# A four-layer graph network on one core: the first pass reordered, and the first norm's squares moved to ScalarE

## The reference

```python
# layer 0: relation weights, every row divided by its norm
rel = adj.T * (q @ k.T);  rel = rel / norm(rel, axis=2);  y = rel @ v
# layer 1: degree-normalised graph convolution
dis = where(deg > 0, rsqrt(deg), 0);  y = (adj * dis[:, None] * dis[None, :]) @ (x @ weight) + bias
# layer 2: gated recurrent update, 3 steps (in_mat = out_mat = adj)
z = sigmoid(w3(av) + u3(h));  r = sigmoid(w4(av) + u3(h))
hv = tanh(w5(av) + u5(r * h));  h = (1 - z) * h + z * hv
# layer 3: attention with 8 heads, masked by adj, output projection
x = layernorm(x + layer(x))          # after each of the four
```

## Time and profile before

| | |
|---|---|
| median of 3 timed executions | 2054.93 us (2052.94 to 2056.11) |
| the profiled execution | 2056.67 us |
| its span, first to last instruction | 2054.8 us |
| mean granted TensorE clock | 0.991 of full speed |
| busy: TensorE, VectorE, ScalarE, GpSimd | 97%, 75%, 62%, 50% |

### The profile page before, as it was taken

The page is one execution under the profiler, slowest core; times in us unless marked ns, Lnnn a source line. Parts: engine busy times, 40 slices in busy tenths (PEclk is TensorE's granted clock), DMA queues, the critical chain, the costliest instruction groups (busy, mean ns, idle before and its releaser), DMA issues.

```text
span 2054.8 us, 34581 instructions
## 1 busy us (share of the span) xinstructions
PE 1998.2 (97%) x12222; PEld 1634.8 (80%) x12222; DVE 1541.4 (75%) x3442; ACT 1277.9 (62%) x2629; POOL 1034.4 (50%) x1153
## 2 busy tenths in 40 slices
PE   6889999999999999999999999999999999999997
PEld 5767888887888878888887888888888887888775
DVE  5557777777777878777777777878777777777867
ACT  3336657576575766657576575766657576575766
POOL 3123645546365554645446365554645446364546
PEclk8999999999999999999999999999999999999999
DMA  4003022130211303122130211303122130211212
GB/s 138 1 21 73 14 60 52 42 73 22 52 42 42 73 21 72 28 56 52 42 73 22 54 40 42 73 22 72 34 50 52 42 73 21 57 37 44 71 41 73
DMA packets 65631, 101.14 MB, mean 49 GB/s; under 512 B 11440, under 2 KB 31152, under 8 KB 65456
## 3 DMA queue, kind: packets, MB, share of 16 engines
q1 hardware_dynamic: 65456, 98.87, 19.0%
HBM read 23.34 MB, written 8.39 MB: 15 GB/s over the span
## 4 chain that ended last, share of the span: by engine, by line
PE 91%; DVE 4%; ACT 3%; issue 1%; DMA 0%; POOL 0%; DVEq 0%; SPq 0%; POOLq 0%; ACTq 0%
PE ps L1066 18%; PE ps L1068 18%; PE ps L1067 17%; PE ps L1088 12%; PE ps L1185 11%; PE ps L1205 6%; PE ps L1169 5%; PE ps L1511 2%; ACT fa L570 1%; PE ps L1267 1%; DVE xn L791 1%; PE ps L1418 1%; PE ps L1359 1%; PE ps L1305 1%; ACT ra L481 0%
## 5 line engine op out<-in xcount | busy, mean ns | idle before, releaser
L341 POOL TENSOR_SCALAR fa<-fa,rsum 128x512 f32<-128x512 f32 x512 | 454.9, 900 | 54.5 <-POOL rsum L335 54.5
L335 POOL TENSOR_TENSOR rsum<-esum,mhalf 128x2 f32<-128x2 f32 x256 | 199.0, 777 | 528.5 <-ACT fa L457 526.8
L817 DVE CUSTOM_DVE_ANT_0 fa<-ps,mask 128x512 f32<-128x512 f32 x512 | 332.1, 686 | 132.4 <-PE ps L1169 130.0
L457 ACT ACTIVATE fa<-fa,nmax 128x512 f32<-128x512 f32 x512 | 367.6, 728 | 27.0 <-DVE nmax L817 27.0
L452 ACT COPY pT<-ps 128x512 f32<-128x512 f32 x480 | 277.0, 584 | 130.6 <-PE ps L1185 130.1
L1185 PE MATMUL ps<-ident,fa 128*128 128x128 f32 x1920 | 287.4, 275 | 7.9 <-ACT pT L452 5.7
L1185 PEld LDWEIGHTS ps<-ident,fa 128*128 128x128 f32 x1920 | 228.8, 140 | 80.6 <-issue 23.8
L804 DVE TENSOR_TENSOR ra<-ps,ra 128x512 fp32r<-128x512 f32 x224 | 151.2, 687 | 161.9 <-ACT ra L608 90.0
L1088 PE MATMUL ps<-adjT,ra 128*128 128x512 f32 x1024 | 253.6, 399 | 3.2 <-DVE ra L959 3.2
L1088 PEld LDWEIGHTS ps<-adjT,ra 128*128 128x128 f32 x1024 | 193.1, 191 | 46.5 <-issue 3.8
L330 POOL TENSOR_TENSOR rstd<-veps,mhalf 128x2 f32<-128x2 f32 x128 | 98.0, 772 | 166.6 <-DVE veps L767 141.5
(11 more groups left out here) (209 smaller groups left out, 4709.6 us busy)
## 6 DMA issues: line engine op xcount, KB each, us to landing
ra<-ra SPq DMA_DIRECT2D x512, 128.0 KB, 2.3
fa<-in_x_T SPq DMA_DIRECT2D x17, 512.0 KB, 4.7
fa<-in_x SPq DMA_DIRECT2D x17, 512.0 KB, 3.9
out<-fa SPq DMA_DIRECT2D x15, 512.0 KB, 3.0
fa<-in_L_gnn_w_w SPq DMA_DIRECT2D x3, 512.0 KB, 9.6
adj_n<-in_adj SPq DMA_DIRECT2D x1, 1024.0 KB, 8.9
fa<-in_L_gnn_u_w SPq DMA_DIRECT2D x2, 256.0 KB, 9.6
out<-xn SPq DMA_DIRECT2D x2, 256.0 KB, 2.1
```

The lines of the kernel that those rows point to most:

```text
L335: nc.gpsimd.tensor_tensor(rsum[:, 2 * k:2 * k + 2], esum[:, 2 * k:2 * k + 2], mhalf[:, 4:6], ALU.pow).then_inc(rs_r, 1)
L341: nc.gpsimd.tensor_scalar(SC[:, g], SC[:, g], rsum[:, 2 * k + u:2 * k + u + 1], 1.0, ALU.mult, ALU.mult).then_inc(nrm, 1)
L457: nc.scalar.activation(SC[:, s % RING], SC[:, s % RING], ACT.Exp, bias=nmax[:, s:s + 1], scale=-1.0, accum_out=esum[:, s:s + 1]).then_inc( ...
L817: nc.vector.tensor_tensor_reduce(out=SC[:, s % RING], in0=ps[:, (4 if i is not None else lone_bank(k)) + u], in1=mask[:, 2 * (k % 8 // 4) ...
```

## The change

It has five parts. (1) `degrees_and_sums()` becomes `degrees()` at the old place and `first_sums()` between `rel_of(0)` and `rel_of(1)`; the difference `st3 - st4` moves to `other_sums()`. (2) `flag_and_degrees()` stands in front of the first norm instead of behind it. (3) The fifth gate weight (`u5`) is transposed, copied and split later, by `gate_weights([4])`: on TensorE behind the `w1` product, on ScalarE and VectorE behind the high and low parts of h. The wait in front of step 0 stays as it is. (4) The first norm is made in the way of the second: `sums_and_means(k, ...)` serves both, with the squares on ScalarE in `centred_squares(k)`. This holds for every pass that carries a graph through layer 0, and it doubles the small tiles `xsum`, `nmean`, `vsum`. (5) In pass 0 the `u5` product of the reset gate is done one column half after the other.

```diff
+            def centred_squares(k):
+                for c in range(2):
+                    act.wait_ge(ln_m[k], i * 2 + (c + 1))
+                    for s in (2 * c, 2 * c + 1):
+                        ins = nc.scalar.activation(XS[:, s], xg[:, s], ACT.Square, bias=nmean[:, k, s:s + 1],
+                                                   scale=ROOT[k], accum_out=vsum[:, k, s:s + 1])
+                    ins.then_inc(ln_q[k], 1)
...
                 if i is not None:
+                    centred_squares(0)
                     for c in range(2):
                         act.wait_ge(x1s_f, i * 2 + (c + 1))
                         copy(XNS[:, H, half(c)], XS[:, half(c)]).then_inc(x1s_h, 1)
                     if i == 0:
-                        gate_weights()
+                        gate_weights(range(4))
...
                     for d in range(DT):
                         act.wait_ge(h_c, i * 2 + (d + 1))
                         copy(HTS[:, H, d], hT[:, d]).then_inc(hT_h, 1)
+                if i == 0:
+                    gate_weights([4])
...
-            def degrees_and_sums():
+            def degrees():
                 prep(nc.vector.reduce_sum(dtmp[:, 0, :], adj_n[:, :, :], AX.X))
                 settled()
                 TS(dtmp[:, 1, :], dtmp[:, 0, :], 1.2e-38, None, ALU.max).then_inc(s_dve, 1)
+
+            def first_sums():
                 dve.wait_ge(w2_in, 16 * 5)
                 prep(TT(st4[:, :, 0:D], st4[:, :, 0:D], st4[:, :, D:2 * D], ALU.add))
                 prep(TT(st3[:, :, 0:D], st3[:, :, 0:D], st3[:, :, D:2 * D], ALU.add))
+
+            def other_sums():
                 settled()
                 dve.sem_inc(s_dve, 1)
                 TT(st3[:, :, 0:D], st3[:, :, 0:D], st4[:, :, 0:D], ALU.subtract).then_inc(s_dve, 1)
-
-            def other_sums():
...
-                def sums_and_statistics(k, ready, scale, x):
+                def sums_and_means(k, ready, scale, x):
                     for c in range(2):
                         dve.wait_ge(ready, i * 2 + (c + 1))
                         for s in (2 * c, 2 * c + 1):
-                            ins = STT(xg[:, s], natural(2)[:, s], scale[:, s:s + 1], x[:, s], ALU.mult, ALU.add)
+                            ins = STT(xg[:, s], natural(2)[:, s], scale[:, s:s + 1], x[:, s], ALU.mult, ALU.add,
+                                      accum_out=xsum[:, k, s:s + 1])
                         after("g", mark("g", ins))
-                        variance("g", k, c, aggregate("g", k, c, stats_of("g", xg, k, c)))
+                        TS(nmean[:, k, half(c)], xsum[:, k, half(c)], -ROOT[k] / D, None, ALU.mult).then_inc(ln_m[k], 1)
                     for c in range(2):
+                        n = mark("g", TS(mv[:, k, half(c), 0], xsum[:, k, half(c)], 1.0 / D, None, ALU.mult))
                     after("g", n)
                     for c in range(2):
+                        dve.wait_ge(ln_q[k], i * 2 + (c + 1))
+                        TS(veps[:, k, half(c)], vsum[:, k, half(c)], (EPS, 0.25 * EPS)[k], None, ALU.add).then_inc(ln_v[k], 1)
...
                     rel_of(0)
                 if t is not None:
                     normalize(x3, xg, 2, 1, t, x3_r)
+                if first:
+                    first_sums()
                 if i is not None:
                     rel_of(1)
...
                     dve.wait_ge(rn_r, i + 1)
                     if first:
+                        flag_and_degrees()
                         dve.wait_ge(s_pool, w1_l + 1)
-                    sums_and_statistics(0, o_ps, rnorm, XIN)
+                    sums_and_means(0, o_ps, rnorm, XIN)
                 if first:
-                    flag_and_degrees()
...
                         TT(HTS[:, L, d], hT[:, d], f32(HTS[:, H, d]), ALU.subtract).then_inc(hT_l, 1)
+                if first:
+                    gate_weights([4])
...
-                    gate_weights()
+                    gate_weights(range(4))
                     pe.wait_ge(s_dve, flag + 1)
                     lo_words = pe.value_load(any_lo[0:1, 0:1])
...
                                 ins.then_inc(o1_ps, 1)
+                if first:
+                    gate_weights([4])
...
+                    if t is None:
+                        pe.wait_ge(rh_l, m + 2)
+                        for q in range(DT):
+                            for d in range(DT):
+                                ins = block_of(0, W["u5"], AB1, q, d, False, d == DT - 1)
+                            ins.then_inc(v_ps, 1)
                     for d in range(DT):
-                        if i is not None:
+                        if i is not None and t is not None:
                             pe.wait_ge(rh_l, m + (d + 1))
                             for q in range(DT):
                                 ins = block_of(0, W["u5"], AB1, q, d, False, d == DT - 1)
```

More of the change, by code:

```diff
@@ L67, in gnn_stack @@
         rstd = sb("rstd", [P, 4, NT])
-        xsum = sb("xsum", [P, NT])
-        nmean = sb("nmean", [P, NT])
-        vsum = sb("vsum", [P, NT])
+        xsum = sb("xsum", [P, 2, NT])
+        nmean = sb("nmean", [P, 2, NT])
+        vsum = sb("vsum", [P, 2, NT])
         rsd = sb("rsd", [P, NT])
@@ L126, in gnn_stack @@
         QK_BANK = (6, 7, 1, 7)
-        CHAIN_G, CHAIN_T, CHAIN_O = 6 + 4 + 2 + 8 * STEPS, 4, 4
+        ROOT = (1.0 / 16, 1.0 / 32)
+        CHAIN_G, CHAIN_T, CHAIN_O = 4 + 4 + 2 + 8 * STEPS, 4, 4
         def pair(b):
@@ L171, in gnn_stack @@
         u_ps = sem("u_ps"); u_h = sem("u_h"); u_l = sem("u_l"); o_ps = sem("o_ps")
-        x2_m = sem("x2_means"); x2_q = sem("x2_squared")
+        ln_m = [sem(f"means_of_norm_{k}") for k in range(2)]
+        ln_q = [sem(f"squares_of_norm_{k}") for k in range(2)]
         ln_v = [sem(f"var_of_norm_{k}") for k in range(4)]
@@ L431, in adjacency, with gate_weights @@
                 copy(adjT[:, H, s], ps[:, ADJ_BANK[s], :]).then_inc(s_act, 1)
-            def gate_weights():
-                for k, name in enumerate(VIA_PSUM):
+            def gate_weights(ks):
+                for k in ks:
+                    name = VIA_PSUM[k]
                     act.wait_ge(s_pe, wt_ps + k + 1)
@@ L566, in body @@
                 if i is not None:
[L567 to L572, removed]
+                    centred_squares(1)
                 if t is not None:
@@ L780, in sums_and_statistics @@
                         for s in (2 * c, 2 * c + 1):
-                            ins = STT(xg[:, s], natural(2)[:, s], scale[:, s:s + 1], x[:, s], ALU.mult, ALU.add)
+                            ins = STT(xg[:, s], natural(2)[:, s], scale[:, s:s + 1], x[:, s], ALU.mult, ALU.add,
+                                      accum_out=xsum[:, k, s:s + 1])
                         after("g", mark("g", ins))
-                        variance("g", k, c, aggregate("g", k, c, stats_of("g", xg, k, c)))
-                def sums_and_means():
+                        TS(nmean[:, k, half(c)], xsum[:, k, half(c)], -ROOT[k] / D, None, ALU.mult).then_inc(ln_m[k], 1)
                     for c in range(2):
[L789 to L796, removed]
+                        n = mark("g", TS(mv[:, k, half(c), 0], xsum[:, k, half(c)], 1.0 / D, None, ALU.mult))
                     after("g", n)
                     for c in range(2):
-                        dve.wait_ge(x2_q, i * 2 + (c + 1))
-                        TS(veps[:, 1, half(c)], vsum[:, half(c)], 0.25 * EPS, None, ALU.add).then_inc(ln_v[1], 1)
+                        dve.wait_ge(ln_q[k], i * 2 + (c + 1))
+                        TS(veps[:, k, half(c)], vsum[:, k, half(c)], (EPS, 0.25 * EPS)[k], None, ALU.add).then_inc(ln_v[k], 1)
                 def tile_lo(dst, b, d, ready, value, signal):
@@ L869, in body @@
                         adjacency(s)
-                    degrees_and_sums()
+                    degrees()
                 if t is not None:
@@ L976, in body @@
                     dve.wait_ge(xb_r, i + 1)
-                    sums_and_means()
+                    sums_and_means(1, o1_ps, dinv, xg)
                 if i is not None:
@@ L1139, in adjacency, with gate_weights @@
                 ins.then_inc(s_pe, 1)
-            def gate_weights():
-                for k, src in enumerate((st4, st3, st5, stu3, stu5)):
+            def gate_weights(ks):
+                for k in ks:
+                    src = (st4, st3, st5, stu3, stu5)[k]
                     pe.wait_ge(s_dve, w2_sum + min(k + 1, 4))
```

## The result

The changed kernel takes 2046.52 us (median of 6, 2045.05 to 2047.54), before 2054.69 us (median of 6). The ratio is 0.9961 with a 95% interval of 0.9951 to 0.9971: 8.2 us less, faster by 0.39%. The prediction had 2049.2 us, a gain of 5.7, in a range of 2045.3 to 2052.6. The profiled execution of the changed kernel took 2046.74 us with a span of 2045.0 us, 9.8 us less than the span before.

What follows compares the result with a forecast made beforehand. TensorE, busy for 97% of the span, was taken to bound the kernel. Minus 6.4, plus 3.7, minus 2.0, minus 1.0 gave minus 5.7 us, so 2049.2 us from the median 2054.93, range 2045.3 to 2052.6.

Steps and rivals of the forecast that it cites:

- The sums ahead: Pass 0: the sums moved ahead of u let the values matmuls start at 32.64 instead of 35.00, 2.36 us earlier.
- The bound of 1.3: Pass 0: if UB's low parts were slowed as L695 was, the sums' term would be 1.3 us instead of 2.4.
- The roots: Before pass 0's first norm: degree roots fit by a tenth of a microsecond; cost 0, at most 0.5 us.
- The shorter norm: First norm with squares on ScalarE: chain 1.0 us shorter in pass 0, and pass 1's 3.2 us wait shrinks by 1.0.
- The first gather: Pass 0: with the fifth weight moved away, the gather starts when x is ready, at 42.45, 6.4 us earlier.
- The fifth weight's wait: Pass 0: step 0's gather still waits for all five low gate weights, so it is held back 3.7 us.
- Rival (a): Before step 0: the fifth weight costs nothing, giving minus 9.4 us, 2045.5 us; chance 0.08.
- The reset gate: Pass 0 steps: u5 by column halves brings the last transposes 0.67 us sooner, 2.0 us over three steps.
- Rival (b): Held gather or step pauses: one or two more 1.2 GHz stretches leave 2.3 to 4.0 us gain; chance 0.22.
- Later passes: Middle passes: the shorter norm chain buys at most 14 times 0.08 us before the gather, taken as 0.
- Rival (c): Middle passes: ScalarE squares hold up each of 14 passes, slower if the chain lengthens by 0.73 us; chance 0.04.
- Rival (d): Pass 0: the moved sums wait for their loads; at 2.5 us late, 2051.6 us remains; chance 0.04.

Runs made afterwards that it cites:

- the wait moved: Changed kernel with TensorE's wait for the fifth low gate weight moved from before step 0's gather to the u5 product: 2044.06 us, again 2043.12 us.
- its repeat: The kernel before, unchanged, run again as a kernel of its own: 2055.64 us, ratio 1.0002 to before.
- kept-busy kernel: Changed kernel with the fifth weight's wait moved, plus matmuls nobody reads in four TensorE pauses: 2039.95 us, against 2043.12 us without those matmuls.

## Why the prediction was right

The sign is right, and so are most of the terms. The total was forecast too small, since two of its terms were.

**The sums ahead** (2.36): 2.34 in the distance from `u` to the values matmuls, in the changed kernel and with parts 1 and 2 alone. The bound of 1.3, if `UB`'s low parts had been slowed, did not come: the pair (28.85) took 1.29 us beside GpSimd's operation at 28.41.

**The roots** (0, at most 0.5): they fitted by 0.2 us where a tenth was foreseen. The sign that the prediction named for late roots, a VectorE wait on GpSimd, did show, 0.74 us long, and cost nothing: what counts is whether it outlasts the wait for the matmuls. **The shorter norm** (1.0): in pass 1 it was 0.98. In pass 0 only 0.4 showed, for the reason given there, the second half of the matmuls; the prediction's 39.8 less 35.7 is 4.1, and 4.04 was measured.

**The first gather** (6.4): 6.45. In both profiles with the wait moved, which are the same kernel up to there, it led by 7.2, since their values matmuls had no stretch at 1.2 GHz; so the fit to a tenth is in part luck. **The fifth weight's wait** (3.7): a pause of 3.50 us, and 3.68 when it was taken away. So the net of part 3 is nothing in the changed kernel, where taking it back changed no time; alone it cost 1.5 us by the medians, with an interval that holds zero. Pass 0 up to step 0 gained 3.06, 2.7 were expected. The held gather took 5.49 us as before (5.50), the first 3.3 of them at 1.2 GHz, so the 1.3 us that half rate throughout would have cost did not come. Rival (a), that the wait is free, is dead: it cost 2.5 to 3.7 us in three comparisons.

**The reset gate** (2.0): ScalarE's tanh starts 0.67 us sooner and step 0 is 0.67 shorter, step 1 0.65. Here the prediction was short. The third step was 2.14 shorter: 0.65 of it is this term, and 1.5 is a stretch at 1.2 GHz that before had behind step 1's pause and the changed kernel has not. The term was sized as a chain of waits, and the shorter pause also spared the clock. Rival (b) had named the clock, but with the wrong sign: it was to take 1.7 us or more, and it gave. This is 1.5 of the missing 2.5 us between 5.7 and 8.2. The parts alone sum to 5.7 us by their medians (2.1, 2.4, 2.7, less 1.5). That this is the prediction's sum is chance: by their ratios they sum to 6.4, each is uncertain by some 2 us, and part 3 is worth another amount alone than with the others. Together they give 8.2 to 8.5, and no surplus over the sum is shown. Between the start and pass 2's gather the profiles have 8 and 6 stretches of 3.4 us at 1.2 GHz in before and its repeat, 6 to 9 in the kernels with one part or two, 5 and 5 in the changed kernel and 4 without part 3 (the twelve matmuls of y left out). What these are worth outside the steps is open; the kept-busy kernel shows that one can be worth 0.3 us and another 1.2.

**Later passes** (0): this is the other term that was too small. The prediction saw 0.08 us to be had in each of 14 passes, 1.1 in all, and put it at nothing without a reason; the gap of 0.08 us ahead of the gather closed, and the middle passes lost 1.0 us together (1.5 to 1.6 from pass 2 on with part 4 alone). Within them about 0.6 us are given back in one pass (at 1026 us), in which a small operation of VectorE took 0.64 us in place of 0.17; such a wait of 0.9 us is in all seven profiles with part 4 and in none without, and its cause is open. The whole rest of the program is 0.17 us longer only by the chance of the last pass. Rival (c) is dead: no middle pass became slower but this one. **Rival (d)**: the sums ran in the hole (18.25 to 19.5 in the changed profile) before the second `rel_of` at 19.82, and no load was late.

The prediction's own range for the likeliest case, 2047.0 to 2050.8, missed 2046.52 by 0.5 us. The wide one held it, but it reached that low for the sake of rival (a), which is not what happened: that the time lies in it is partly luck.

## What to carry to other kernels

When an operation is moved later, look for every wait that counts it, not only for the instruction that reads it: a counting semaphore that is waited for as a whole hands the delay to work that needs none of it. Here the wait stood in front of a gather that reads no weight, and moving it by some lines was worth as much as all the care in placing the fifth weight. And where TensorE pauses for one to three microseconds in a stretch with little work, size the pause twice, as time and as clock: here, by the profiles, work that nobody reads, put into such pauses, took 1.5 us off a step of pass 0 and 1.2 us off pass 1, with no dependence changed (the timed medians show the second kernel's gain and not the first's). It pays only where TensorE itself is what the next stage waits for; ahead of the first gather of pass 0 it gave 0.3 us.

A view of waits leaves the smallest ones out. Where an edit acts in every pass, measure the length of a pass before and after, over many passes: here 0.1 us a pass came to as much as the 1.0 us that pass 1's wait gave up.

## What the runs showed of the hardware

In the first 16 us of a profile the column PEclk can say 1.00 while matmuls of 512 columns start 0.43 us apart; the same twelve matmuls took 2.8 us in one execution and 5.2 in another of one program. With the landing of the loads this moves the start of `u` from 22.1 to 25.7 us, more than any one part of this change is worth. In the last pass, the six profiles with two stretches of 3.4 us at a granted clock of 0.50 between 1960 and 1990 us took 168.1 to 168.5 us from pass 15's gather on, the six with one took 166.8 to 167.2, whatever the kernel. Executions of the changed kernel lay up to 4.3 us apart on one chip; how much of that is the start or the last pass is not shown. The Trainium skill (TensorE: Matmul & The Clock Gate, What's actually happening) says that the monitor runs free of the kernel; the same twelve matmuls at one clock in one execution and at the other in the next (2.8 and 5.2 us) agree.
